# Attention scores on 32 array rows in interleaved row groups, expert rows of 20 token blocks summed by GpSimd, 20 blocks ahead of the experts

## The reference

```python
xn = _layernorm(x)
x = x + attention(xn) + ffn(xn)

# attention: 16 heads of 16 features; a token sees the 128 tokens before it
scores = einsum('bhnqd,bhnkd->bhnqk', qb, kb) * scale
attn = softmax(where(allowed, scores, NEG)); local = attn @ vb
# remote: 4 heads of 16 over 64 pooled chunk means, softmax, then @ rout_w
gate = sigmoid(local @ gl_w + remote_h @ gr_w)
out = (gate * local + (1 - gate) * remote_h) @ out_w + out_b

# ffn: 64 experts of 256 -> 128 -> 256, 8 a token, plus one shared expert
tidx, tw = _gate(x, gate_w, gate_bias)          # top 8 of 64, in 4 of 8 groups
y = sum over experts e: w[:, e] * ((silu(x @ We_gate[e]) * (x @ We_up[e])) @ We_down[e])
y = y + (silu(x @ Ws_gate) * (x @ Ws_up)) @ Ws_down
```

## Time and profile before

| | us |
|---|---|
| median of 3 runs | 1333.56 (1332.71 to 1335.41) |
| the profiled execution, its own time | 1338.67 |
| its span, first to last instruction | 1336.9 |
| TensorE busy, weight loads busy | 1255.4, 1182.4 |
| DVE busy | 953.3 |
| ACT busy | 861.7 |
| POOL busy | 638.7 |

### The profile page before, as it was taken

The page is one execution under the profiler, slowest core; times in us unless marked ns, Lnnn a source line. Parts: engine busy times, 40 slices in busy tenths (PEclk is TensorE's granted clock), DMA queues, the critical chain, the costliest instruction groups (busy, mean ns, idle before and its releaser), DMA issues.

```text
span 1336.9 us, 38681 instructions
## 1 busy us (share of the span) xinstructions
PE 1255.4 (94%) x9266; PEld 1182.4 (88%) x9267; DVE 953.3 (71%) x4532; ACT 861.7 (64%) x2383; POOL 638.7 (48%) x747
## 2 busy tenths in 40 slices
PE   4957999999999989999999999999999999999996
PEld 3956999999999979999999999999988999999985
DVE  6776666666666637667676676765559898989897
ACT  2323877777777856556565566566657777777774
POOL 7803777777777726565565665656650000000000
PEclk9678999999999979999999999999999999999998
DMA  8107455544333337777777777775545333333330
GB/s 255 63 1 280 163 185 188 206 163 162 123 118 112 114 120 223 211 233 223 224 232 212 233 226 214 233 215 170 175 139 218 107 106 106 106 109 113 116 119 19
DMA packets 152813, 218.40 MB, mean 163 GB/s; under 512 B 24769, under 2 KB 124866, under 8 KB 147650
## 3 DMA queue, kind: packets, MB, share of 16 engines
q1 hardware_dynamic: 80450, 86.77, 20.4%
q0 software_dynamic: 28800, 86.54, 16.9%
q10 hardware_dynamic: 43520, 44.57, 13.1%
HBM read 113.86 MB, written 103.81 MB: 163 GB/s over the span
## 4 chain that ended last, share of the span: by engine, by line
PE 73%; DVE 12%; issue 6%; DMA 3%; ACTq 2%; ACT 2%; DVEq 1%; SPq 1%
PE psS L951 19%; PE psS L824 10%; PE psT L935 5%; PE psO L960 5%; PE psT L838 4%; PE psM L960 4%; DVE x_all L1604 4%; DMA pr<-slot_rows 2%; PE psQ L771 2%; PE psV L811 2%; PE psV L782 2%; PE psQ L792 2%; PE psT L852 2%; PE psT L851 2%; PE psT L850 1%
## 5 line engine op out<-in xcount | busy, mean ns | idle before, releaser
L951 PEld LDWEIGHTS psS<-sm,wt 128*128 128x128 f32 x2560 | 310.8, 193 | 19.5 <-issue 7.8
L951 PE MATMUL psS<-sm,wt 128*128 128x128 f32 x2560 | 316.6, 277 | 1.7 <-ACT sm L1210 0.7
L636 POOL DMA_INDIRECT slot_rows<-x_out_st,idx_st x256 | 257.0, 1004 | 77.5 <-issue 68.6
L1116 ACT ACTIVATE pr<-sm,nmax 128x192 f32<-128x192 f32 x512 | 205.1, 449 | 54.5 <-DVE nmax L1544 52.7
L824 PE MATMUL psS<-kT,qz 128*128 128x192 f32 x1024 | 225.2, 343 | 10.8 <-DVE qz L1487 8.4
L663 POOL DMA_INDIRECT home_rows<-qz,row_idx x160 | 154.6, 966 | 131.0 <-DVE qz L1637 103.4
L663 POOL DMA_INDIRECT home_rows<-sm,row_idx x160 | 155.3, 971 | 86.4 <-issue 45.0
L1228 ACT COPY wt<-shared_mem 128x512 f32 x320 | 183.4, 627 | 4.8 <-issue 4.8
L1216 ACT ACTIVATE prT<-psS 128x256 f32<-128x256 f32 x160 | 61.6, 385 | 187.7 <-issue 100.0
L824 PEld LDWEIGHTS psS<-kT,qz 128*128 128x128 f32 x1024 | 164.3, 192 | 18.4 <-issue 10.3
L1544 DVE CUSTOM_DVE_ANT_0 sm<-psS,pr 128x192 f32<-128x192 f32 x512 | 162.0, 353 | 18.5 <-issue 14.6
(11 more groups left out here) (283 smaller groups left out, 2492.6 us busy)
## 6 DMA issues: line engine op xcount, KB each, us to landing
shared_mem<-home_rows SPq DMA_DIRECT2D x32, 1024.0 KB, 5.1
pr<-slot_rows ACTq DMA_DIRECT2D x120, 272.0 KB
qz<-slot_rows ACTq DMA_DIRECT2D x40, 272.0 KB
slot_rows<-wt SPq DMA_DIRECT2D x32, 272.0 KB
shared_mem<-in_L_ffn_We_gate SPq DMA_DIRECT2D x64, 128.0 KB
shared_mem<-in_L_ffn_We_up SPq DMA_DIRECT2D x64, 128.0 KB
shared_mem<-in_L_ffn_We_down SPq DMA_DIRECT2D x64, 128.0 KB
x_all<-in_L_attn_x SPq DMA_DIRECT2D x4, 1024.0 KB, 9.1
```

The lines of the kernel that those rows point to most:

```text
L636: pool.indirect_dma_start(slot_rows, bass.IndirectOffsetOnAxis(ap=idx_st[:, j, k:k + 1], axis=0), x_out_st[:, j % 2, :], None).then_inc(sc ...
L951: last = mm(psS[:, j % 2, (2 * a + n) * P:(2 * a + n + 1) * P], wt[j % 2][:, a, c, n * F:(n + 1) * F], xsT[:, j % 2, a, c, :], start=(c == ...
L1116: nc.scalar.activation(pr[:, p % 4, par, :], sm[:, p % 4, par, :], ACT.Exp, bias=nmax[:, p % 4, par:par + 1], scale=-1.0).then_inc(probs, 1)
```

## The change

Three things change together.

1. `qz` shrinks from eight copies of a query to two (`own_half` instead of `own_head`). A score matmul contracts over the 32 partitions on which its two heads lie (`qz[r, ...]`, `kT[r, ...]`), so that it uses one 32-row group of the array. `scores` runs at even steps only and issues two pairs, their matmuls alternating between two row groups and the two banks; it waits until both earlier pairs are masked. DVE masks both pairs at even steps.
2. The expert rows of the blocks before FIRST (past) are summed by GpSimd, in five `tensor_tensor` operations a block: one multiplication of 128x2048 by the weights, and additions of 1024, 512, 256 and 256 columns. The rows of the others (own) are added by DVE, each block's during its own attention, eight additions a block, before `accumulate`. SP has two buffers for past blocks and three for own ones, and handles both in one written-out order: two past blocks for each own block.
3. FIRST goes from 17 to 20: 20 blocks of attention ahead of the experts and 12 behind. The experts' buffers get memory of their own (`more_mem`).

```diff
-FIRST = NB // 2 + 1
+FIRST = 20
+OWN_ROWS, PAST_ROWS = 3, 2
...
-        qz = sb("qz", [P, DC, 2, HPC, UQ])
+        qz = sb("qz", [P, DC, 2, 2, UQ])
...
+            load_past(0)
+            load_own(FIRST)
+            load_past(1)
+            load_own(FIRST + 1)
+            load_own(FIRST + 2)
+            announce_own(FIRST)
+            for n in range(NB - FIRST):
+                t = FIRST + n
+                if n:
+                    sp.wait_ge(combined, n)
+                    if t + 2 < NB:
+                        load_own(t + 2)
+                if t + 1 < NB:
+                    announce_own(t + 1)
+                if n >= 3:
+                    store_own(t - 3)
+                for m in (2 * n, 2 * n + 1):
+                    if m < FIRST:
+                        store_past(m)
...
+            def store_past(t):
+                sp.wait_ge(past_combined, t + 1)
+                if t + PAST_ROWS < FIRST:
+                    load_past(t + PAST_ROWS)
+                sp.dma_start(yt[:, t, :], x_all[:, t, :]).then_inc(stored, 16)
...
+            def combine_past(j, t, g):
+                pool.wait_ge(rows_ready[j], 16 * (g + 1))
+                row = rows_in[:, j, :, :]
+                nc.gpsimd.tensor_tensor(row, row, w8[:, t, :].unsqueeze(2).broadcast_to([P, K, D]), ALU.mult).then_inc(past_steps, 1)
+                for n, k in enumerate((K // 2, K // 4, K // 8)):
+                    pool.wait_ge(past_steps, 4 * t + n + 1)
+                    nc.gpsimd.tensor_tensor(row[:, 0:k, :], row[:, 0:k, :], row[:, k:2 * k, :], ALU.add).then_inc(past_steps, 1)
+                pool.wait_ge(past_steps, 4 * t + 4)
+                nc.gpsimd.tensor_tensor(x_all[:, t, :], x_all[:, t, :], row[:, 0, :], ALU.add).then_inc(past_combined, 1)
...
                 if p >= 2 or nth:
-                    pe.wait_ge(masked, 2 * (n - 1))
-                heads = slice(p % PPC * 2, p % PPC * 2 + 2)
+                    pe.wait_ge(masked, 2 * n)
                 for u in range(2):
-                    last = mm(psS[:, p % 2, u * WIN:(u + 1) * WIN], qz[:, c, u, heads, :].rearrange("p h t -> p (h t)"),
-                              kT[:, c, u * UQ:u * UQ + WIN], start=True, stop=True)
-                last.then_inc(s_ready, 1)
+                    for m in (p, p + 1):
+                        r = slice(m % PPC * 2 * HD, (m % PPC + 1) * 2 * HD)
+                        last = mm(psS[:, m % 2, u * WIN:(u + 1) * WIN], qz[r, c, u, :, :].rearrange("p h t -> p (h t)"),
+                                  kT[r, c, u * UQ:u * UQ + WIN], start=True, stop=True)
+                        if u == 1:
+                            last.then_inc(s_ready, 1)
...
-                    if live:
+                    if live and s % 2 == 0:
                         scores(i, s, nth)
...
-            def accumulate(i):
+            def accumulate(i, combining):
                 dve.wait_ge(out_ready, i + 1)
+                if combining:
+                    dve.wait_ge(combined, i - FIRST + 1)
...
-                    if combining:
-                        add_row(i, 2 * s + 1)
+                    if combining and live and resuming and s >= NPAIR - K // 2:
+                        for k in range(2):
+                            add_row(i, 2 * (s - NPAIR) + K + k)
+                    if combining and live and not resuming:
+                        add_row(i, s)
```

More of the change, by code:

```diff
@@ L203, in build @@
               [sm_mem[:, n * 2 * D:(n + 1) * 2 * D] for n in range(2)] +
-              [more_mem[:, 4 * D + n * 2 * D:4 * D + (n + 1) * 2 * D] for n in range(2)]]
+              [more_mem[:, 2 * ROW + n * 2 * D:2 * ROW + (n + 1) * 2 * D] for n in range(2)]]
         xsT = sm_mem[:, 4 * D:8 * D].rearrange("p (j a c t) -> p j a c t", j=2, a=2, c=DC)
@@ L340, in build @@
         idx_ready = sem("idx_ready")
-        rows_ready = [sem(f"rows_ready{j}") for j in range(ROWS)]
+        rows_ready = [sem(f"rows_ready{j}") for j in range(OWN_ROWS + PAST_ROWS)]
         rows_landed = sem("rows_landed")
@@ L476, in announce_rows, with store_own @@
                 sp.sem_inc(rows_landed, 1)
-            def store_block(t):
-                sp.wait_ge(combined, t + 1)
+            def store_own(t):
                 sp.wait_ge(acc_done, t + 1)
                 sp.dma_start(yt[:, t, :], x_all[:, t, :]).then_inc(stored, 16)
[L483 to L492, removed]
@@ L493, in _ @@
-            for j in range(ROWS):
-                store_block(NB - ROWS + j)
+            def store_past(t):
[9 more added lines that the diff above has]
+            announce_own(FIRST)
@@ new lines, in _ @@
+            for n in range(NB - FIRST):
[11 more added lines that the diff above has]
+                        store_past(m)
+            for t in range(NB - 3, NB):
+                store_own(t)
@@ L668, in _ @@
                     send_home(j, g * YS + j)
+            def combine_past(j, t, g):
[7 more added lines that the diff above has]
+                nc.gpsimd.tensor_tensor(x_all[:, t, :], x_all[:, t, :], row[:, 0, :], ALU.add).then_inc(past_combined, 1)
+            pool.wait_ge(weights_kept, 1)
+            pool.wait_ge(acc_done, FIRST)
+            with pool.Fori(0, FIRST // PAST_ROWS) as g:
+                for j in range(PAST_ROWS):
+                    combine_past(j, g * PAST_ROWS + j, g)
         @block.tensor
@@ L1586, in body, with add_row @@
                         latent_out(i)
[L1587 to L1605 removed]
+                    if combining and live and resuming and s >= NPAIR - K // 2:
[3 more added lines that the diff above has]
+                        add_row(i, s)
+            def add_row(t, k):
+                n = t - FIRST
+                if k == 0:
+                    dve.wait_ge(rows_landed, n + 1)
+                else:
+                    dve.wait_ge(combine_steps, (K - 1) * n + k)
+                row = rows_in[:, bass.ds(PAST_ROWS + t % OWN_ROWS, 1), k, :].rearrange("p a d -> p (a d)")
+                ins = v.scalar_tensor_tensor(x_all[:, t, :], row, w8[:, t, k:k + 1], x_all[:, t, :], ALU.mult, ALU.add)
+                ins.then_inc(combine_steps if k < K - 1 else combined, 1)
             def attention(start, end, combining):
```

64 lines of the change are left out of this document (22 added, 42 removed).

## The result

| | before | after |
|---|---|---|
| median, us | 1334.49 (1332.71 to 1336.76, 4 runs) | 1403.18 (1399.01 to 1410.93, 4 runs) |
| ratio after / before | | 1.0521, 95% interval 1.0469 to 1.0572 |
| profiled execution, its span | 1338.67, 1336.9 | 1399.01, 1397.2 |
| mean granted TensorE clock | 0.973 | 0.929 |

The change makes the kernel 5.2% slower; the forecast was 1371 us, the range 1285 to 1425. The page of after first: the busy time of the engines, and the slices of TensorE and of its clock in tenths, as in the earlier trace rows.

The account below looks back on a forecast made before the run. TensorE was taken to bound blocks ahead of the experts, with DVE on the chain behind. 22.5 us more ahead plus 15 behind made 37.5 on the profiled 1338.7, 1376.2, less 5.1 to the median: 1371 us, range 1285 to 1425.

Parts of the forecast that it names:

- What bounds the kernel before: TensorE alone sets the pace ahead of the experts, 21.03 us a block; behind them the chain changes over to DVE, 21.65.
- Part 1, the scores: Attention blocks: two pairs' scores in 32-row groups take 3.8 us a block instead of 5.86.
- the loads' end: Bound for two pairs' scores if only weight loads remain in a row: 0.89 us for eight records; 0.90 was taken.
- the block of 19.0: Attention block with the new scores: 21.03 - 5.86 + 3.8 = 19.0 us, ends 18.0 and 20.6.
- rival (c): Row groups bring nothing: no overlap, 1413 us, or TensorE emptying at each change, up to 2.2 us a block, 1426; chance 0.20.
- ACT 16.4, DVE 12.3, both fit in 19.0: ACT's 16.4 us of work a block and DVE's 13.9 less 1.6 both fit in a block of 19.0 us.
- Part 2, 20 blocks ahead: Stage ahead of the experts: 20 x 19.0 + 6.3 = 386.3 us, 22.5 more than before; the scatter stays hidden.
- rival (d): TensorE's clock falls to half in gaps behind the experts, adding between nothing and 40 us, up to 1411 us; chance 0.07.
- Part 3, turns of GpSimd and DVE: Behind the experts the two alternate operations, each holding the other: about 30 us a block for ten blocks, 15 us more.
- (a): Rival: GpSimd and DVE don't block each other; 234 us behind the experts, total 1253 us, faster; chance 0.14.
- (b): Rival: GpSimd's long operations let DVE in between, only port time adds up; 271 us behind the experts, 1290 total; chance 0.12.

## Why the forecast was right on the sign and 32 us short

- **What bounds the kernel before**: held. All that was gained or lost lies in the two stages, but for the 7.6 us by which the first score came earlier and the 1.8 in the experts. The change needn't have a part in the 7.6: before's own trace from another chip has its first score at 107.9, after's is at 107.2.
- **Part 1, the scores, 3.8 us a block**: 3.5, a little better than the loads' end. But the block of 19.0 us missed two things. The transposes behind each piece take 0.15 longer, 4 x 0.15 = 0.6 (it may be the price between row layouts of rival (c), at a quarter of its 2.2; no run tells it apart). With 5.86 - 3.5 - 0.6 = 1.8 less the block should be 19.2, and it is 19.28 with the latent step early. What the argument "ACT 16.4, DVE 12.3, both fit in 19.0" failed on is the wait for ACT's copy in step 7: busy time doesn't show that an operation stands behind others in its queue. The late copy costs 20.25 - 19.28 = 0.97 us a block by the two runs, 0.52 of it in TensorE's idle time in front of L912.
- **Part 2, 20 blocks ahead, +22.5**: +57.4. 20 x (20.25 - 19.0) = 25.0 of the missing 34.9; the other 9.9 are, but for 0.6, four blocks of 21.3 to 23.6 us in which the clock had fallen, all gone in the run with the latent step early. So rival (d), given behind the experts alone, acted ahead of them too. The scatter stayed hidden (454 us).
- **Part 3, turns of GpSimd and DVE, +15**: +12.4, ten blocks of 30 us as forecast, and holds of the length of GpSimd's operation, with maxima of 3.8 us instead of "above 4". The mechanism is shown three ways: no hold without GpSimd's sums, none beside fills, shorter ones beside shorter operations. But the total came out by terms that offset each other. GpSimd took 3.72 us for its product of 2048 columns, not 4.53 (its sum of 1024 columns took 2.42, where 2.36 was worked out), and 179 us in all instead of 227; and it stood idle for 84 us, which the sum didn't have, waiting for loads. SP issues these behind `combined`, and spent 208 us of the stage waiting for DVE's row sums there; a landing of 5.1 us beside the other buffer's 10.0 didn't cover that. And 13.7 us a block at half clock, which the sum put at nothing, can be worth up to half of the 9.95 us that TensorE was busy in them. The blocks ended at 22.8 and 20.0 instead of two of 19. That this stage came out within 3 us of its forecast is luck.
- **The rivals**: (a) and (b) are out, by e.g. 3.82 us for a row sum that starts 0.33 behind GpSimd's product. With short operations, where no row sum takes over 1.05 us, the stage falls to 1336.2 - 1050.2 = 286.0 us; (b) gave 271 for after. (c) is out: 0.85 us a quad. (d) was right in kind, and was given too little.

The step that failed is thus the block ahead of the experts: 19.0 was forecast as if TensorE alone stayed on the chain, and it was 20.25, and more where the clock fell.

## What to carry to other kernels

When the engine that bounds a loop is relieved, walk through the other engines' queues in order, not only their busy sums: look for the one operation that stands behind work that isn't due, and move it ahead; here it cost 0.97 us in each of 20 blocks and some 10 us more by falls of the clock. Work handed to GpSimd that reads SBUF should come in short operations where DVE has operations with two SBUF inputs beside it: the hold is the length of the operation under way. And a handed-over part pays only if the receiving engine's own time, here 11.5 us twice a block, stays under the block.

## What the runs showed of the hardware that was not expected

- GpSimd's float32 product of 2048 columns, with the weights broadcast as its second input, took 3.60 to 3.87 us, 1.76 ns a column at the least, where 4.53 us was worked out; its sum of 1024 columns took 2.42 us, close to the 2.36 worked out. Cut into 256 columns a product took 0.70 us beside DVE.
- A fill by GpSimd (1.79 us) held DVE's copy of the masks up to 2.13 us, though it held no row sum (0.486 at most).
- Score products over 32 rows took 0.85 us for eight records, where over 128 rows they took 1.30 to 1.46, in alternation or not.
- TensorE's waits of 0.26 and 0.52 us in step 7 went with 6.8 us at half clock a block (0.86 granted), which made the block 2.4 us longer than the 21.5 with the latent step early (1.00). They don't do it every time: in the first run of the scores part alone, three blocks with the same 0.26 and 0.52 took 21.5 us each at 0.99, and then, with nothing changed in the kernel, all others 23.8 at 0.86. In after, with 0.52 in front of L912, the clock fell twice in the 20 blocks ahead of the experts. What decides isn't shown.
- Two chips ran the same kernel before in 1587 and 1565 us instead of 1334; on the second, whose trace stands above, the loss lies ahead of and in the experts (a chain piece of 5.2 us with no known cause among it), and none behind them.
